# Attention over the batch: the output projection as three rounded passes over pairs of groups, with the result and the output weights split in high and low parts

## The reference

```python
def _L1_attn_ref(h, Wq, Wkv, Wo):
    N_HEAD, D_HEAD = 16, 64
    L, B, _ = h.shape                                  # 16, 128
    q = (h @ Wq).reshape(L, B, N_HEAD, D_HEAD)
    k, v = jnp.split(h @ Wkv, 2, axis=-1)              # each reshaped as q
    score = jnp.einsum('ibnd,jbnd->ijbn', q, k) * scale
    prob = jax.nn.softmax(score, axis=1)
    vec = jnp.einsum('ijbn,jbnd->ibnd', prob, v).reshape(L, B, N_HEAD * D_HEAD)
    return vec @ Wo                                    # (.., 1024) @ (1024, 128)
```

## Time and profile before

| | us |
|---|---|
| median of 3 runs (780.96 to 782.8) | 781.2 |
| the profiled execution, device time | 781.81 |
| its span, first to last instruction | 779.9 |
| busy in the span: PE, PEld | 634.5, 460.4 |
| busy in the span: DVE, ACT, POOL | 460.8, 377.6, 266.1 |

### The profile page before, as it was taken

One profiled execution on the slowest core, in us unless ns is written; L12 is line 12 of the kernel. 1 busy time (PEld: TensorE's weight loads), 2 busy tenths in 40 slices (PEclk: granted clock), 3 DMA queues, 4 the chain that ended last, 5 costly groups with the idle time before them and its releaser, 6 DMA issues. The chain is left out here.

```text
span 779.9 us, 17100 instructions
## 1 busy us (share of the span) xinstructions
PE 634.5 (81%) x6403; PEld 460.4 (59%) x6435; DVE 460.8 (59%) x1247; ACT 377.6 (48%) x817; POOL 266.1 (34%) x369
## 2 busy tenths in 40 slices
PE   3799998988999974348999985989999997685776
PEld 2455555555666553325999952667878685363555
DVE  3466655478788865752444325475757573555994
ACT  5566674868676722125444465635353523323342
POOL 3133223344344210752455562041313131143641
PEclk9799999999999995555999997999999999556898
DMA  3022344333112111116466622300000000000000
GB/s 101 2 60 67 85 103 128 90 95 78 52 40 83 62 41 46 49 42 198 169 215 216 221 54 56 86 1 2 2 2 3 1 3 2 0 1 0 8 20 27
DMA packets 53023, 48.95 MB, mean 63 GB/s; under 512 B 10219, under 2 KB 45533, under 8 KB 52685
## 3 DMA queue, kind: packets, MB, share of 16 engines
q1 hardware_dynamic: 46925, 41.09, 17.7%
q0 software_dynamic: 2496, 4.27, 1.7%
q10 hardware_dynamic: 3520, 2.50, 1.2%
HBM read 18.68 MB, written 15.54 MB: 44 GB/s over the span
## 5 line engine op out<-in xcount | busy, mean ns | idle before, releaser
L573 ACT ACTIVATE ptx<-bank 128x512 f32<-128x512 f32 x128 | 66.1, 602 | 90.7 <-PE bank L486 90.6
L1576 POOL COPY ptx<-over_pt 32x512 f32<-32x512 f32 x64 | 39.0, 610 | 132.9 <-DVE over_pt L1546 130.1
L1141 POOL DMA_INDIRECT results<-moe_y,moe_dest x46 | 45.3, 984 | 59.1 <-DVE moe_y L1279 51.1
L386 POOL TENSOR_TENSOR x<-x,l_back 128x128 f32<-128x128 f32 x32 | 14.6, 456 | 125.0 <-ACT l_back L586 113.9
L727 DVE SCALAR_TENSOR_TENSOR ptx<-ptx,bank 128x512 f32<-128x512 f32 x64 | 41.1, 684 | 25.5 <-PE bank L495 23.7
L482 PE MATMUL bank<-ke 32*128 32x512 f32 x256 | 37.4, 652 | 18.6 <-issue 14.9
L712 DVE TENSOR_REDUCE l_m<-bank 128x4 f32<-128x512 f32 x64 | 40.9, 679 | 19.4 <-PE bank L470 19.4
L1476 ACT ACTIVATE ke<-bank 64x512 f32<-64x512 f32 x64 | 38.0, 593 | 15.1 <-PE bank L1407 14.2
L1136 POOL DMA_INDIRECT slots<-xs,moe_pos x32 | 32.3, 1010 | 28.7 <-DVE moe_pos L1222 18.6
L712 DVE TENSOR_REDUCE l_m_raw<-bank 128x4 f32<-128x512 f32 x64 | 40.7, 674 | 0.1
L1450 PE MATMUL bank<-over_ot,over_wo 128*128 128x128 f32 x256 | 34.4, 290 | 6.0 <-DVE over_ot L1552 6.0
(11 more groups left out here) (347 smaller groups left out, 1662.4 us busy)
## 6 DMA issues: line engine op xcount, KB each, us to landing
slots<-blank SPq DMA_DIRECT2D x16, 528.0 KB, 4.7
ptx<-w SPq DMA_DIRECT2D x12, 578.0 KB
ke<-w SPq DMA_DIRECT2D x11, 578.0 KB, 3.3
w<-in_w SPq DMA_DIRECT2D x16, 256.0 KB
moe_xb<-slots SPq DMA_DIRECT2D x23, 132.0 KB
x<-in_x SPq DMA_DIRECT2D x4, 256.0 KB, 5.3
w<-results SPq DMA_DIRECT2D x4, 256.0 KB, 6.0
w<-results ACTq DMA_DIRECT2D x4, 256.0 KB, 5.8
```

What stands on the lines that cost most here:

```text
L573: nc.scalar.activation(probs[t % 2][:, g, :], score_bank[g][:, :], ACT.Exp, scale=SCALE0).then_inc(s["probs"], 1)
L1141: nc.gpsimd.indirect_dma_start(M.results, bass.IndirectOffsetOnAxis(dest[j % 4][:, n:n + 1], 0), y[j % 4][:, n, :], None, bounds_check=2 * ...
L1576: nc.gpsimd.tensor_copy(ptx[t % 2][r, :, r], pt[t % 2][r, :, :]).then_inc(s["spread"], 1)
```

## The change

1. The output projection is done for a pair of groups `u` (two groups side by side, 256 columns) in step `t = 2u+4`, every other step, where before each group had its own in step `t+3`. It is 24 `float32r` passes of 256 columns: for each of eight weight blocks, high weights by high result, high by low, low by high.
2. `ot` becomes `ot_hi` and `ot_lo` (two buffers each, each for a pair). `weighted(t)`: ACT copies both `o_bank`s, rounded, into `ot_hi`; DVE then subtracts `ot_hi` from both `o_bank`s into `ot_lo`, each after ACT's copy of the same bank.
3. ACT rounds `over_wo` to `wo_hi` ahead of its first step; DVE makes `wo_lo` by a subtraction at the end of its step 0.
4. The copy to `yt_all` takes 256 columns for a pair.
5. The mask tile `rows` is made 32 wide and broadcast when read; four small tiles are laid into `head_ones`.

```diff
                 def values(t):
...
-                    wait(pe, s["o0"], t)
-                    wait(pe, s["o1"], t)
+                    wait(pe, s["o_lo"], t, per=2)
...
-                def result(t):
-                    pe.wait_ge(s["o0"], t + 1)
-                    pe.wait_ge(s["o1"], t + 1)
-                    wait(pe, s["y"], t)
+                def result(u):
+                    if u == 0:
+                        pe.wait_ge(s["wo_lo"], 1)
+                    wait(pe, s["o_lo"], u, per=4, plus=4)
+                    wait(pe, s["y"], u)
+                    o = y_bank[:, 0:2 * S]
                     for r in range(PAIR):
-                        mm = nc.tensor.matmul(y_bank[:, 0:S], wo[:, r, :], ot[t % 2][:, r, :], start=r == 0, stop=r == PAIR - 1)
+                        nc.tensor.matmul(o, wo_hi[:, r, :], ot_hi[u % 2][:, r, :, :], start=r == 0, stop=False)
+                        nc.tensor.matmul(o, wo_hi[:, r, :], ot_lo[u % 2][:, r, :, :], start=False, stop=False)
+                        mm = nc.tensor.matmul(o, wo_lo[:, r, :], ot_hi[u % 2][:, r, :, :], start=False, stop=r == PAIR - 1)
                     mm.then_inc(s["y_ps"], 1)
...
-                    if 0 <= t - 3:
-                        result(t - 3)
+                    if t >= 4 and t % 2 == 0:
+                        result(t // 2 - 2)
...
                 def weighted(t):
                     act.wait_ge(s["o_ps"], t + 1)
-                    wait(act, s["y_ps"], t, plus=-1)
-                    nc.scalar.activation(ot[t % 2][:, 4:8, :], o_bank[1][:, :].rearrange("p (r q) -> p r q", r=4), ACT.Copy).then_inc(s["o1"], 1)
+                    wait(act, s["y_ps"], t // 2, plus=-1)
+                    for n in range(2):
+                        nc.scalar.activation(ot_hi[t // 2 % 2][:, 4 * n:4 * n + 4, t % 2, :], o_bank[n][:, :].rearrange("p (r q) -> p r q", r=4),
+                                             ACT.Copy).then_inc(s["o_hi"], 1)
...
                 def weighted(t):
-                    dve.wait_ge(s["o_ps"], t + 1)
-                    wait(dve, s["y_ps"], t, plus=-1)
-                    nc.vector.tensor_copy(ot[t % 2][:, 0:4, :], o_bank[0][:, :].rearrange("p (r q) -> p r q", r=4)).then_inc(s["o0"], 1)
+                    wait(dve, s["y_ps"], t // 2, plus=-1)
+                    for n in range(2):
+                        dve.wait_ge(s["o_hi"], 2 * t + n + 1)
+                        part = slice(4 * n, 4 * n + 4)
+                        nc.vector.tensor_tensor(ot_lo[t // 2 % 2][:, part, t % 2, :], o_bank[n][:, :].rearrange("p (r q) -> p r q", r=4),
+                                                ot_hi[t // 2 % 2][:, part, t % 2, :].bitcast(F32), ALU.subtract).then_inc(s["o_lo"], 1)
...
+                    if t == 0:
+                        dve.wait_ge(s["wo_hi"], 1)
+                        nc.vector.tensor_tensor(wo_lo[:, :, :], M.over_wo[:, :, :], wo_hi[:, :, :].bitcast(F32), ALU.subtract).then_inc(s["wo_lo"], 1)
```

More of the change, by code:

```diff
@@ L1360, in batch_attention @@
         s = semaphores(nc, "over", """masks ring_ps q ke v0 v1 s_ps top less exps sums inv scaled turned spread
-            o_ps o0 o1 y_ps y cosine""")
+            o_ps o_hi o_lo y_ps y cosine wo_hi wo_lo""")
         PAIR, HB, G, QUADS = H // 2, 64, S // 8, 4
-        hi, lo, wo, ke, ptx, yt = M.over_hi, M.over_lo, M.over_wo, M.ke, M.ptx, M.yt_all
+        hi, lo, ke, ptx, yt = M.over_hi, M.over_lo, M.ke, M.ptx, M.yt_all
         xhi, xlo = (t[:, :, :].rearrange("p s b -> p (s b)") for t in (M.over_xhi, M.over_xlo))
@@ L1368, in batch_attention @@
         pt = two("pt", [S, H, 32])
-        ot = two("ot", [128, PAIR, S])
-        top, sums, inv = sb("top", [S, H, 1]), sb("sums", [S, H, 1]), sb("inv", [S, H, 1])
-        side, rows = sb("side", [128, S], BF16), sb("rows", [128, H, 32], BF16)
+        wo_hi, wo_lo = sb("wo_hi", [128, PAIR, D], F32R), sb("wo_lo", [128, PAIR, D], F32R)
+        ot_hi, ot_lo = [[sb(f"ot_{part}{n}", [128, PAIR, 2, S], F32R) for n in range(2)] for part in ("hi", "lo")]
+        top, sums, inv = [M.head_ones[:, n:n + H].rearrange("p (h a) -> p h a", a=1) for n in (64, 64 + H, 64 + 2 * H)]
+        side, rows = M.head_ones[:, 0:64].bitcast(BF16), sb("rows", [128, 1, 32], BF16)
         ring, s_bank, o_bank, y_bank = M.bank[0:3], M.bank[3:5], M.bank[5:7], M.bank[7]
@@ L1423, in scores @@
                     o = s_bank[t % 2]
-                    nc.tensor.matmul(o[:, :], side[:, :], rows[:, :, :], start=True, stop=False, skip_group_check=True)
+                    nc.tensor.matmul(o[:, :], side[:, :], rows[:, :, :].broadcast_to([128, H, 32]), start=True, stop=False, skip_group_check=True)
                     for r in range(PAIR):
@@ L1488, in weighted, with result @@
                     act.wait_ge(s["o_ps"], t + 1)
-                    wait(act, s["y_ps"], t, plus=-1)
-                    nc.scalar.activation(ot[t % 2][:, 4:8, :], o_bank[1][:, :].rearrange("p (r q) -> p r q", r=4), ACT.Copy).then_inc(s["o1"], 1)
-                def result(t):
-                    act.wait_ge(s["y_ps"], t + 1)
-                    nc.scalar.activation(yt[:, 8 * t:8 * t + 8, :], y_bank[:, 0:S].rearrange("p (s i) -> p s i", i=B),
+                    wait(act, s["y_ps"], t // 2, plus=-1)
+                    for n in range(2):
+                        nc.scalar.activation(ot_hi[t // 2 % 2][:, 4 * n:4 * n + 4, t % 2, :], o_bank[n][:, :].rearrange("p (r q) -> p r q", r=4),
+                                             ACT.Copy).then_inc(s["o_hi"], 1)
+                def result(u):
+                    act.wait_ge(s["y_ps"], u + 1)
+                    nc.scalar.activation(yt[:, 16 * u:16 * u + 16, :], y_bank[:, 0:2 * S].rearrange("p (s i) -> p s i", i=B),
                                          ACT.Copy).then_inc(s["y"], 1)
+                nc.scalar.activation(wo_hi[:, :, :], M.over_wo[:, :, :], ACT.Copy).then_inc(s["wo_hi"], 1)
                 for t in range(G + 3):
@@ L1508, in _ @@
                         weighted(t - 2)
-                act.wait_ge(s["y"], G)
+                act.wait_ge(s["y"], G // 2)
             @block.vector
@@ L1549, in weighted @@
                 def weighted(t):
-                    dve.wait_ge(s["o_ps"], t + 1)
-                    wait(dve, s["y_ps"], t, plus=-1)
-                    nc.vector.tensor_copy(ot[t % 2][:, 0:4, :], o_bank[0][:, :].rearrange("p (r q) -> p r q", r=4)).then_inc(s["o0"], 1)
+                    wait(dve, s["y_ps"], t // 2, plus=-1)
[4 more added lines that the diff above has]
+                                                ot_hi[t // 2 % 2][:, part, t % 2, :].bitcast(F32), ALU.subtract).then_inc(s["o_lo"], 1)
                 nc.vector.tensor_copy(side[:, :], M.over_sidef[:, :]).then_inc(s["masks"], 1)
-                nc.vector.tensor_scalar(rows[:, :, :], M.over_rowf[:, :].rearrange("p (a k) -> p a k", a=1).broadcast_to([128, H, 32]),
-                                        -BIG, None, ALU.mult).then_inc(s["masks"], 1)
+                nc.vector.tensor_scalar(rows[:, 0, :], M.over_rowf[:, :], -BIG, None, ALU.mult).then_inc(s["masks"], 1)
                 for t in range(G + 3):
```

## The result

The changed kernel takes 791.0 us (median of 4 runs, 790.2 to 793.8) against 781.2: ratio 1.0127, 95% interval 1.0098 to 1.0156. Forecast were 789.9 us and 784 to 800. The profiled execution took 791.55 us against 781.81, 9.7 more.

The account below looks back on a forecast made before the run. PE looked like the bound, with DVE within 0.23 us a step of it. Start 0, loops 2.4, block boundaries 1.2, drain 3.4 and its clock 1.7 sum to 8.7 us: 781.2 becomes 789.9, range 784 to 800.

Parts of the forecast that it names:

- The new projection: PE's output projection for a pair: 24 passes at 0.115 us, 2.76 us instead of 3.60, saving PE 0.84 us.
- rival 3: A pass costs more than its columns: 22 us more (812), or 36 more (826) with weight loads unhidden; chance 0.03.
- What DVE and ACT get: Per group, DVE's one copy becomes two subtractions of 692 ns; ACT has two rounding copies of 597 ns instead of one.
- The loop: Inside a block, from one pair's projection to the next: 14.05 us against 13.25, 0.80 more, three times, 2.4 us.
- Across a block boundary: From projection 1 to 2 and 3 to 4: 27.13 us against 26.54, 0.59 more, twice, 1.2 us.
- The start: The first steps, with low weights and subtractions added and step 3's projection gone: between -0.8 and +1.1 us, 0 taken.
- The drain: The last steps, from projection in step 14 to the last `yt_all` copy: 28.34 us against 24.94, 3.4 more.
- the clock term: In the drain, PE idles some 3.2 us before projection 6 and its clock may halve: 1.7 us, ends 0 and 5.
- Rival 1: In the batch attention PE stays the bound and its saving shows: 6.7 us less, 774.5; chance 0.09.
- Rival 2: The clock falls at each PE idle time of 1.6 to 1.8 us: 8.5 us more, 798.4, up to 803; chance 0.07.
- Rivals 3 and 4: The fourth: unseen slack takes up the loop's 0.8 us and the drain's waits, time within 0.3% of before; chance 0.04.

Follow-up runs that it names:

- 16 passes: The changed kernel with the pass of low weights by high result left out, 16 passes a pair instead of 24: ratio 1.0006 to the kernel before.
- double copy: The kernel before with DVE's copy of its half of the result done twice, once into a spare tile: ratio 1.0082 to the kernel before.
- half subtraction: The changed kernel with DVE's subtractions over half the columns of each bank, the 24 passes kept: ratio 0.9968 to the kernel before.
- later projection in the drain alone: The changed kernel with the projection issued after the values of the same step only in steps 16 and 18: ratio 1.0099 to the kernel before.

## Why the prediction was right

- *The new projection*: 24 passes of 0.115 us forecast, 0.12 measured, 2.88 us instead of 2.76. The weight loads, 24 of 0.19 us, are hidden in it, which they could not be by the rule of rival 3. A pass of 256 columns costs half of one of 512 (0.23 us), within 0.005 us.
- *What DVE and ACT get*: 692 and 597 ns forecast, 674 and 595 measured; two subtractions in a row take 1.25 us from first start to last end, where the sum had 1.31.
- *The loop*: 0.80 us a pair forecast, 0.82, 0.87 and 0.88 measured (14.07, 14.12, 14.13), together 2.6 for 2.4. The 16 passes and the double copy each moved it by what the chain says, the half subtraction by 0.2 to 0.3 us more than I had read from it.
- *Across a block boundary*: 27.13 forecast, 27.31 and 27.32 measured, 1.5 for 1.2.
- *The start*: between -0.8 and +1.1 forecast, 0 taken, 0.6 measured. (The working shows 0.4 for DVE, 524.3 against 524.7; the 0.8 for PE stands there without one.) The scores of the second block come 51.25 us after the first matmul, 0.6 more than before. Ahead of values(1), where I had looked for it, the clock stayed up; it fell at the first block start behind 1.91 us of idle time. In the kernel with the later projection in the drain alone, whose first steps are the same, it did not fall, and these steps took 49.87 us, 0.8 less than before.
- *The drain*: 3.4 us plus 1.7 for the clock forecast, 5.5 measured. Projection 6 and values(14) took 1.7 us more than at full clock (4.30 us instead of 2.88, and 2.21 instead of 1.97), which leaves 3.8 for the waits. That the clock term came out to the tenth is luck: it was one value between the ends 0 and 5, and the same kernel, run again, had the clock down twice and 1.5 us more.
- The sum is 0.6 + 2.6 + 1.5 + 5.5 = 10.2 us against 8.7 forecast. The stage is 10.2 longer, the execution 9.7; of the difference 0.4 lies ahead of the block, whose first matmul starts at 486.25 us instead of 486.68.

Every term but the two prices of DVE and ACT came out a little longer than forecast, 1.5 us in all, and the loop, the waits and the idle times stand where the forecast has them.

Rival 1 (PE stays the bound) was wrong by the place: PE is the bound only when the projection stands behind the values; then the pair takes 12.64 us, near the 12.4 of that rival. Rival 2 was wrong for the idle times of 1.5 us and partly right for the long ones. Rivals 3 and 4 did not show.

## What to carry to other kernels

Before work is moved from one engine to another, close the loop: follow one round from an instruction to itself over all engines, with the waits, and see how much slack each engine's chain has; here it was 0.23 us of 6.63, at 59% busy. Work that saves PE time can still lose if it adds to an engine whose step ends by releasing PE. And the place of an instruction in its engine's list is part of its cost: nothing that another engine waits for should stand behind work that nobody needs yet.

## What the runs showed that I had not expected

The clock behind an idle time of PE is not decided by the length of that idle time alone. Ahead of values(1) PE idles 2.46 us in the repeated changed kernel and in the one with 16 passes; the values then run at half clock in the first and at full clock in the second:

```profile
515.34 3.59 PE L1440 MATMUL bank<-ptx,over_v 128*64 128x128 f32 x32 [2.46 <-POOL ptx L1591]
```

```profile
520.47 1.97 PE L1440 MATMUL bank<-ptx,over_v 128*64 128x128 f32 x32 [2.46 <-POOL ptx L1590]
```

The first block start of the changed kernel, and of the one with the later projection in the drain, is a second such couple, a longer record being one at half clock:

```profile
524.59 0.69 PE L1406 MATMUL bank<-over_xhi,over_hi 128*128 128x512 f32 x1 [1.91 <-DVE over_q L1529]
```

```profile
518.34 0.50 PE L1406 MATMUL bank<-over_xhi,over_hi 128*128 128x512 f32 x1 [1.91 <-DVE over_q L1533]
```

After 3.34 and 3.95 us the clock was down both times, in the kernel before and in the one with the double copy. After 2.90 us ahead of projection 6 it went down in all three profiles (changed, changed again, 16 passes), but after 2.99 us ahead of values(14) it stayed up, in the run with the later projection in the drain. From 1.9 to 2.5 us it went both ways. Behind the 1.5 us in the loops and the 1.4 to 1.7 us ahead of a block's first scores it stayed up in every profile. What tells the cases between apart stays open. In the profiles it moves an execution by 1 to 3 us. In the experiments the runs of one kernel spread by 3 to 7.5 us (772.2 to 779.7 in the 24 runs of the kernel before on the second chip), and how much of that is the clock was not taken apart; with 16 passes the fastest run, 781.06 us, had a mean granted clock of 0.895 and the slowest, 786.89, one of 0.885.
